# One-hots of every third tile made by ScalarE, and another order of the node products, in a graph layer

## The reference

```python
h = relu(layernorm(x))
skip_s, skip_v = s(h) @ W_skip0, v(h) @ W_skip1          # per node
s1, v1 = s(h) @ W_nl0, v(h) @ W_nl1
w = relu(edge_feat @ W_fc1) @ W_fc2                      # per edge, 224 weights
tp = products of w, s1[dst], v1[dst], direction          # per edge
agg = segment_sum(tp, src) / 32                          # per node
out_s = agg_s @ W_out_s + skip_s
out_v = agg_v @ W_out_v + skip_v
out = x + [silu(out_s[:, :64]), sigmoid(out_s[:, 64:]) * out_v]
```

## Time and profile before

| | us |
|---|---|
| median of 3 runs (1141.44 to 1143.91) | 1142.42 |
| profiled execution | 1140.97 |
| its span, first to last instruction | 1139.1 |
| PE busy | 1092.1 (96%) |
| DVE busy | 978.3 (86%) |
| ACT busy | 865.4 (76%) |
| POOL busy | 777.3 (68%) |

### The profile page before, as it was taken

One profiled execution on the slowest core, in us unless ns is written; L12 is line 12 of the kernel. 1 busy time (PEld: TensorE's weight loads), 2 busy tenths in 40 slices (PEclk: granted clock), 3 DMA queues, 4 the chain that ended last, 5 costly groups with the idle time before them and its releaser, 6 DMA issues.

```text
span 1139.1 us, 29582 instructions
## 1 busy us (share of the span) xinstructions
PE 1092.1 (96%) x8847; PEld 930.7 (82%) x8847; DVE 978.3 (86%) x3574; ACT 865.4 (76%) x2069; POOL 777.3 (68%) x1021
## 2 busy tenths in 40 slices
PE   6889899999999999888899999999999999999996
PEld 5667688888888888777788888888888888888885
DVE  9999889888888898776498998999989989899974
ACT  0400377877877877555899999999999999999994
POOL 6777777777777777776456767666676666767650
PEclk9899899999999999788799999999999999999998
DMA  9999545555545675334578887878888878887863
GB/s 340 403 404 402 207 130 139 138 139 138 137 140 137 211 239 149 110 113 116 176 291 283 298 288 287 291 290 288 300 288 287 290 289 289 300 289 287 290 217 110
DMA packets 108460, 271.13 MB, mean 238 GB/s; under 512 B 13573, under 2 KB 51751, under 8 KB 108364
## 3 DMA queue, kind: packets, MB, share of 16 engines
q1 hardware_dynamic: 87852, 233.20, 58.3%
q0 software_dynamic: 19200, 36.48, 10.5%
q10 hardware_dynamic: 1312, 0.29, 0.1%
HBM read 126.91 MB, written 143.01 MB: 237 GB/s over the span
## 4 chain that ended last, share of the span: by engine, by line
PE 82%; DVE 8%; issue 3%; DMA 3%; POOL 2%; ACT 0%; SPq 0%; ACTq 0%; DVEq 0%; POOLq 0%
PE bank L1482 18%; PE bank L1495 12%; PE bank L1474 11%; PE bank L1411 6%; PE bank L1486 6%; PE bank L1440 4%; PE bank L1344 4%; PE bank L1312 3%; PE bank L1428 3%; PE bank L1424 3%; PE bank L1426 3%; PE bank L1448 2%; PE bank L1394 2%; DVE bin_hot L644 2%; DVE rank_junk L717 2%
## 5 line engine op out<-in xcount | busy, mean ns | idle before, releaser
L1261 ACT ACTIVATE nn<-xb,n_bias,n_rstd 128x160 f32<-128x160 f32 x784 | 344.9, 522 | 0.0
L530 POOL DMA_INDIRECT slots<-msg,sidx x200 | 209.8, 1049 | 68.3 <-issue 55.0
L979 DVE BATCH_NORM_STATS2 n_stat<-xb 128x6 f32<-128x160 f32 x784 | 195.2, 310 | 12.4 <-DMA xb<-x 10.9
L1070 DVE SCALAR_TENSOR_TENSOR ob<-sg,bank 128x128 f32<-128x128 f32 x588 | 131.9, 279 | 58.3 <-ACT ob L1276 57.2
L1495 PE MATMUL bank<-mg,hot 64*128 64x192 f32 x1568 | 171.8, 338 | 3.1 <-DVE hot L1055 3.1
L514 POOL DMA_INDIRECT xg<-x,dst_i x136 | 135.6, 997 | 44.1 <-issue 42.0
L1268 ACT ACTIVATE nt<-bank 128x640 f32<-128x640 f32 x196 | 137.7, 703 | 33.1 <-PE bank L1475 25.4
L579 POOL TENSOR_TENSOR n_rstd<-n_sum,neg_half 128x8 f32<-128x8 f32 x94 | 156.5, 1665 | 7.6 <-POOL n_sum L572 6.9
L1474 PE MATMUL bank<-ident,nn 128*128 128x128 f32 x784 | 146.8, 310 | 2.6 <-ACT nn L1261 2.6
L1077 DVE TENSOR_TENSOR ob<-ob,xb 128x1280 f32<-128x1280 f32 x98 | 146.3, 1493 | 3.4
L1474 PEld LDWEIGHTS bank<-ident,nn 128*128 128x128 f32 x784 | 109.0, 207 | 47.0 <-issue 46.3
(11 more groups left out here) (194 smaller groups left out, 2680.5 us busy)
## 6 DMA issues: line engine op xcount, KB each, us to landing
xb<-x SPq DMA_DIRECT2D x97, 640.0 KB, 5.2
out_dram<-ob SPq DMA_DIRECT2D x97, 640.0 KB, 3.3
slots<-blank SPq DMA_DIRECT2D x14, 2744.0 KB
mg<-slots SPq DMA_DIRECT2D x98, 392.0 KB, 4.0
messages<-msg SPq DMA_DIRECT2D x50, 382.8 KB
ef<-edge_feat_t SPq DMA_DIRECT2D x50, 125.0 KB, 2.3
slots<-msg,sidx POOLq DMA_INDIRECT x200, 3.8
xg<-x,dst_i POOLq DMA_INDIRECT x136, 6.7
```

The costliest lines, as they stand in the source:

```text
L530: pool.indirect_dma_start(slots[:, :], bass.IndirectOffsetOnAxis(ap=sidx[:, m:m + 1], axis=0), msg[:, c, t, 0:MW], None).then_inc(e_sc[c], 16)
L979: done = dve.bn_stats(n_stat[:, u // U, u % U * G + g, :], xb[:, u, g, :])
L1261: last = act.activation(nn[:, u % 2, h, spread_of(g % 4)], xb[:, u, g, order_of(g % 4)], ACT.Relu, bias=n_bias[:, u // U, c:c + 1], scale= ...
```

## The change

Three parts. **Binning:** the one-hots of tiles t >= 54 with t divisible by 3 are made by ScalarE: |iota - bin| into a small ring `bin_far`, then relu(weight - weight * that) into `bin_hot`, with a wait for its own first step between. TensorE waits for `b_lit` for these tiles and counts `b_hot` for the others. ScalarE's calls (`lights`) are spread between its other work, and the zero copies to `msg` are moved behind the first group's normalisation, one between every three tiles. `s_half` is merged into `s_blank`.

**Nodes, TensorE:** `skip` is split into the long products (`skip`) and the short ones (`skip_z`). A round becomes turn(i, 1), skip(i, 0), turn(i+1, 0), skip_z(i, 0), add(i, 0), skip_z(i, 1), add(i, 1), skip(i, 1). In half 1 the short products open the sums and the long ones end them.

**Nodes, ScalarE:** `evacuate(i + 1, 0)` goes ahead of `gates(i, 0)`. The copy of half 0 waits for the short products of the macro-tile before (`n.last`), that of half 1 for `n.z`.

```diff
             place -= XO
             return xb[:, place // 2, place % 2 * GE:place % 2 * GE + GE, :]
+        def on_scalar(t):
+
+            return t >= LIT and t % 3 == 0
+
+        def lit_by(t):
+
+            return len([k for k in range(t + 1) if on_scalar(k)])
+
+        def hot_by(t):
+            return t + 1 - lit_by(t)
+
         def within(q):
             return 0 <= q < NG
...
-                pool.wait_ge(s_half, 1)
+                pool.wait_ge(s_blank, 3)
...
-                dve.memset(neg_half[:], -0.5).then_inc(s_half, 1)
+                dve.memset(neg_half[:], -0.5).then_inc(s_blank, 1)
...
-                    if t + AHEAD < NT:
+                    if t + AHEAD < NT and not on_scalar(t + AHEAD):
...
                     act.dma_start(to, of).then_inc(s_w, 16)
                 act.wait_ge(s_tab, 1)
                 act.activation(vec_r[:], vec_d2[:], ACT.Sqrt).then_inc(s_sqrt, 1)
-                act.wait_ge(s_blank, 2)
-                for c in range(MR):
-                    last = act.activation(msg[96:P, c, :, :], blank[96:P, :].rearrange("p (t c) -> p t c", t=GE), ACT.Copy)
-                last.then_inc(s_msgpad, 1)
+                act.wait_ge(b_hot, 1)
+                act.activation(weight_neg[:], weight[:], ACT.Copy, scale=-1.0).then_inc(b_far, 1)
+
+                def lights(first, last):
+
+                    for t in range(first, last):
+                        if on_scalar(t):
+                            k = lit_by(t)
+                            act.wait_ge(b_pre, t - BR + 4)
+                            act.activation(bin_far[:, k % 2, :], iota_bin[0:ET, :], ACT.Abs, bias=bin_of[:, t:t + 1],
+                                           scale=-1.0).then_inc(b_far, 1)
+                            act.wait_ge(b_far, k + 1)
+                            act.activation(bin_hot[:, t % BR, :], bin_far[:, k % 2, :], ACT.Relu, bias=weight[:, t:t + 1],
+                                           scale=weight_neg[:, t:t + 1]).then_inc(b_lit, 1)
+
                 act.wait_ge(s_w, 16 * len(weight_loads))
                 act.activation(fwd[:, SG:WA + WZ], fwd[:, SG:WA + WZ], ACT.Copy, scale=0.5).then_inc(s_fwd, 1)
+                lights(LIT, 66)
                 act.activation(wo_s[:], wo_s[:], ACT.Copy, scale=1.0 / 32.0)
                 act.activation(wo_u[0:S, :], wo_u[0:S, :], ACT.Copy, scale=3.0 ** 0.5 / 64.0)
                 act.activation(wo_u[S:S + V, :], wo_u[S:S + V, :], ACT.Copy, scale=1.0 / 64.0)
                 act.activation(wo_u[S + V:S + 2 * V, :], wo_u[S + V:S + 2 * V, :], ACT.Copy, scale=1.5 ** 0.5 / 64.0)
+                lights(66, 75)
                 for j in range(2):
                     same, cross = slice(2 * V * j, 2 * V * j + V), slice(2 * V * j + V, 2 * V * j + 2 * V)
                     act.activation(wo_v[same, :], wo_v[same, :], ACT.Copy, scale=1.0 / 64.0)
...
                         last.then_inc(e_norm, 1)
                 root_e(0)
-                norm_e(0, range(GE))
+                lights(75, 96)
+                norm_e(0, range(0, 2))
+                lights(96, 99)
+                norm_e(0, range(2, GE))
+                lights(99, 102)
                 act.wait_ge(s_mir, 1)
                 act.activation(rev[:], p_rev, ACT.Copy).then_inc(s_rev, 1)
+                act.wait_ge(s_blank, 2)
+                for c in range(MR):
+                    lights(102 + 3 * c, 105 + 3 * c)
+                    last = act.activation(msg[96:P, c, :, :], blank[96:P, :].rearrange("p (t c) -> p t c", t=GE), ACT.Copy)
+                last.then_inc(s_msgpad, 1)
                 act.wait_ge(e_t, 1)
                 act.activation(ht[:, 0, :, :], f_t, ACT.Copy).then_inc(e_ht, 1)
+                lights(126, 147)
                 act.wait_ge(e_h1, 1)
                 act.activation(hid[:], f_h, ACT.Relu).then_inc(e_hid, 1)
+                lights(147, 165)
                 act.wait_ge(e_w, 1)
                 act.activation(w_sb[:, 0, :, :], f_w, ACT.Copy).then_inc(e_wsb, 1)
+                lights(165, NT)
                 def round_e(q):
                     c = q % 2
...
                     def evacuate(i, h):
                         act.wait_ge(n.t, 2 * i + h + 1)
-                        wait(act, n.z, 2 * i + h - 1)
+                        if h == 0:
+                            wait(act, n.last, 4 * (i - 1) + 2)
+                        else:
+                            wait(act, n.z, 2 * i)
                         act.activation(nt[:, h, :], q_t[h], ACT.Relu).then_inc(n.ht, 1)
                     def gates(i, u, h):
...
                         evacuate(i, 1)
                         if macro_exists(i + 1):
                             norm(i + 1, (u + 1) % XU, 1)
-                        gates(i, u, 0)
                         if macro_exists(i + 1):
                             evacuate(i + 1, 0)
+                        gates(i, u, 0)
                         if macro_exists(i + 2):
                             norm(i + 2, (u + 2) % XU, 0)
...
                 count(2, ones_h, 1)
                 count(2, tri_before, 2).then_inc(b_pre, 1)
                 for t in range(NT):
-                    if t + 3 < NT:
-                        pe.wait_ge(b_hot, t + 4)
+                    if t + 3 < NT and on_scalar(t + 3):
+                        pe.wait_ge(b_lit, lit_by(t + 3))
+                    elif t + 3 < NT:
+                        pe.wait_ge(b_hot, hot_by(t + 3))
                     pe.wait_ge(b_rank, t + 1)
                     if t + 3 < NT:
                         count(t, tri_rest, t)
...
                         pe.transpose(q_t[h][:, 4 * P:5 * P], nn[:, u % 2, h, LAST], ident[:]).then_inc(n.t, 1)
                     def skip(i, h):
-                        z = q_z[h]
                         pe.wait_ge(n.ht, 2 * i + h + 1)
                         wait(pe, n.mul, 2 * i + h - 1)
                         for t in range(4):
-                            pe.matmul(z[:, t, 0:F], nt[:, h, t * P:(t + 1) * P], sides[t // 2][:, skip_cols], start=(t % 2 == 0),
-                                      stop=False, skip_group_check=True)
+                            last = pe.matmul(q_z[h][:, t, 0:F], nt[:, h, t * P:(t + 1) * P], sides[t // 2][:, skip_cols],
+                                             start=(h == 0 and t % 2 == 0), stop=(h == 1), skip_group_check=True)
+                        return last
+
+                    def skip_z(i, h):
+                        pe.wait_ge(n.ht, 2 * i + h + 1)
+                        wait(pe, n.mul, 2 * i + h - 1)
                         for j in range(2):
                             part = slice(HALF * j, HALF * j + HALF)
-                            pe.matmul(z[:, 2 * j:2 * j + 2, F:Z], nt[part, h, 4 * P:5 * P], sides[j][part, skip_z_cols],
-                                      start=False, stop=every, skip_group_check=True)
+                            pe.matmul(q_z[h][:, 2 * j:2 * j + 2, F:Z], nt[part, h, 4 * P:5 * P], sides[j][part, skip_z_cols],
+                                      start=(h == 1), stop=every, skip_group_check=True).then_inc(n.last, 1)
                     def add(i, u, h):
                         pe.wait_ge(n.hot, i + 1)
...
                             slots = slice(CAP * (t // 2), CAP * (t // 2) + CAP)
                             pair = 2 * h + t % 2
                             last = pe.matmul(q_z[h][:, t, 0:Z], hot[slots, u % 2, pair, :], mg[slots, u % U, pair, 0:Z],
-                                             start=False, stop=True, skip_group_check=True)
-                        last.then_inc(n.z, 1)
+                                             start=False, stop=(h == 0), skip_group_check=True)
+                        return last
                     def add_every(i):
...
                     turn(0, 0, 0)
                     def round_n(i, u):
+
                         turn(i, u, 1)
                         skip(i, 0)
-                        if not every:
-                            add(i, u, 0)
                         if macro_exists(i + 1):
                             turn(i + 1, (u + 1) % XU, 0)
-                        skip(i, 1)
+                        skip_z(i, 0)
+                        if not every:
+                            add(i, u, 0).then_inc(n.z, 1)
+                        skip_z(i, 1)
+                        if not every:
+                            add(i, u, 1)
+                        last = skip(i, 1)
                         if every:
                             add_every(i)
                         else:
-                            add(i, u, 1)
+                            last.then_inc(n.z, 1)
                     macros(pe, round_n)
```

More of the change, by code:

```diff
@@ L49, in gnn_layer @@
     BR, AHEAD, ACCS = 20, 6, 3
+    LIT = 54
     MW = 196
@@ L210, in gnn_layer @@
         s_held = sem("s_held")
-        s_half = sem("s_half")
         b_hot = sem("b_hot")
+        b_far = sem("b_far")
+        b_lit = sem("b_lit")
         b_pre = sem("b_pre")
```

(1 more changed line is left out.)

2 lines of the change are left out of this document (added).

## The result

The changed kernel takes **1112.63 us** (median of 4 runs, 1111.03 to 1115.19) against 1141.93 for the kernel before on the same chip (1139.14 to 1143.91): a ratio of 0.9747, 95% interval 0.9717 to 0.9778. The forecast was 1119, in a band of 1113 to 1130, with a range of 1108 to 1134. The profiled execution took 1114.05 us, its span is 1112.2. A second measurement on another chip gave 1116.91 beside 1142.17, ratio 0.9760 (0.9733 to 0.9787); what lies between the two is taken up with the experiments.

A forecast was written before the change was run, and what follows sets the result against it. GpSimd's transfers bound the edge stage's end, TensorE the node stage, next the loads of x. Savings of 18.5, 2.4, about 2 and 0.7 us, together 23.6, off 1140.97 gave 1117.4, against the median 1119; range 1108 to 1134.

The forecast's parts named there:

- The bound of the edge stage: Edge stage: its end hangs on GpSimd's count of transfers, 1.33 us each, not on when binning ends.
- Zero was the term: Binning: 0 us of the 12 us taken off VectorE reach the total; plus or minus 3 us for TensorE's clock.
- TensorE's gain: Node stage: one change into and out of half-height products per macro-tile instead of two, 0.30 us saved, 5.59 us left.
- I take a value between, 0.30 us: Node stage, TensorE: saving per macro-tile chosen between 0.24 us and the weight loader's standing still, 0.40 us a half.
- The sum of 0.24: Node stage, TensorE: lower bound of the saving, 0.10 us into the K=64 products plus 0.14 out of them.
- the ring: Node stage: residual, load of x, statistics, residual; 11.18 us for two macro-tiles, 5.59 to 5.67 each, 5.64 taken.
- Rival A: Node stage: the ring never binds, loads land in 4.9 us or overlap better, TensorE sets the pace; 1105 to 1113, 13%.
- C: Node stage: the ring lengthens, landings 5.4 to 5.5 us or issue held back, 5.75 to 5.83 a macro-tile; 1130 to 1137, 13%.
- D: Node stage: slower, the ring stays at 6.13 us a macro-tile as in the early stretch; 1155 us, 8%.
- ScalarE's order: Node stage: moving the copy ahead of half 0's gates and its new waits cost zero; if any, 0.1 us a macro-tile.
- The rate of transfers: Node stage: at 358 GB/s a macro-tile's transfers take an estimated 4.8 us and bind nothing; the trace shows delay, not rate.

The follow-up runs named there:

- binning alone: Only the binning hunks of the change, put on the kernel before, nodes in the old order: 1141.56 us, ratio 0.9983.
- both further edits: Changed kernel with VectorE's statistics five macro-tiles ahead, not six, and GpSimd taking three gathers a round, not two: 1087.57 us; with the old binning 1087.1.
- the ring open: Changed kernel with VectorE taking node statistics five macro-tiles ahead instead of six (five-ahead), loads issued as before: 1098.82 us, ratio 0.9598.

## Why the prediction was right

**The bound of the edge stage: right.** 151 one-hots are left on VectorE, the last rank starts at 113.6 us, the last gather goes out at 481.21. VectorE's waits for gathered rows grew from 15.3 us to 23.7 in the same stretch; they took up most of what binning gained. The lines (GpSimd's timeline, then groups by line as the earlier trace rows):

```profile
481.21 0.97 POOL L530 DMA_INDIRECT xg<-x,dst_i  x1 [0.30 <-issue]
```

```profile
L672 DVE BATCH_NORM_STATS2 e_stat<-xg 125x6 f32<-125x160 f32 x136 | 36.9, 311 | 23.7 <-DMA xg<-x,dst_i 23.7
```

This isn't chance: the waits are 15.0 to 19.5 us in four kernels with the old binning, 23.7 to 27.8 in seven with the new. Zero was the term, and two comparisons bear it out: binning alone, and both further edits with and without it. But GpSimd's count tells the last gather, not the end: behind it the last 40 scatters took 4 to 11 us more than GpSimd's own 53, and the end moved with that, about as far as the prediction's plus or minus 3 us allowed. One size was off besides: a pair of ScalarE's activations was put at 1.2 us (bounds 1.0 to 1.4). It takes 0.93, by the starts of two pairs in ScalarE's timeline:

```profile
85.35 0.44 ACT L1191 ACTIVATE bin_far<-iota_bin,bin_of 125x196 f16<-125x196 f16 x1
85.83 0.55 ACT L1194 ACTIVATE bin_hot<-bin_far,weight,weight_neg 125x196 f16<-125x196 f16 x1
86.28 0.44 ACT L1191 ACTIVATE bin_far<-iota_bin,bin_of 125x196 f16<-125x196 f16 x1
```

The nearest row, a normalisation of 160 columns, was too dear a model for it. The estimate of 0.89 us from the Trainium skill (ScalarE: Activation LUTs, "What ACT_TABLE_LOAD costs") is the nearer one. Following or ignoring the Trainium skill's advice to leave such work to VectorE (same page, "Rules for kernel authors") made no difference to the time, 1087.1 and 1087.57 us, as the trace's view of a free engine had it.

**TensorE's gain: right in kind, undersized.** The step that failed is "I take a value between, 0.30 us: not all of the loader's standing delays a product". All of it does: 0.40 measured, and 0.40 a half was the loader's waiting. The sum of 0.24 from the earlier trace rows had two of the four places, the step into the short products and the slow first products behind the adds. It missed the first short product's own delay, and the adds' last step was named there but given too little. TensorE alone makes 5.47 us, outside the 5.49 to 5.65 given for it. Had the ring not bound, this step would have cost the forecast its range: with the ring open the kernel takes 1098.82.

**The ring: right, and it is why the error above cost little.** The prediction took 5.64 between the ring's terms (5.59 to 5.67). It gave TensorE 5.59 too, so that the number alone couldn't have told the two apart; the runs with the ring open and lengthened do. The period was 5.626 and 5.651 in two profiles, with VectorE waiting for x in 43 and 52 of 76 macro-tiles, near the "last about half the time" of the prediction. TensorE's true 5.47 is hidden behind it. The middle macro-tiles gave 0.267 each instead of 0.25, the last ten 0.27 each where eight at 0.30 stood, the first 16 and the start 3.1 us together where 2.7 stood. Rival A failed on the other condition: the loads land in 5.15 us, not in 4.9, and hence TensorE's speed can't show. Its time, 1105 to 1113, holds the measured 1112.6 all the same, by another path: a ring at 5.63 plus 2 us of the edge stage. Rivals C and D needed landings over 5.4 us; the medians stayed at 5.15 and 5.2. The one edit that did lengthen the landing, the load put first, lengthens the period as C had it, to 5.719.

**From 1119 to 1112.6.** The node stage gave 24.9 us of span against 23.6 forecast. The edge stage's end added 2.0 where zero, plus or minus 3, was written; in the second measurement, with a first `mg` load at 549.70, the whole gain was 25.3 us. Another 2.4 is the choice of the profiled execution: before, it lay 1.0 below the median that the changed kernel is compared with, after, 1.4 above its own. The last half us is that median itself, 1141.93 where the forecast started from 1142.42. So some 5 of the 6 us come from the edge stage's end and from which executions are compared, not from the node stage.

**ScalarE's order: half right.** Little is late that wasn't before: between 650 and 1080 us the copy waits 3.3 us in 9 places for the short products, and TensorE's long products 3.0 us in 13 for VectorE's gate products, where zero was put. With the ring open neither wait is left. That the place itself may bring 0.05 to 0.07 us a macro-tile was not seen.

**The rate of transfers.** The Trainium skill's 358 GB/s (DMA: Bandwidth & Descriptors, "Specifications") is not contradicted: the five-ahead kernel moves 306 GB/s from 650 to 1080 us. But by that rate nothing would have waited for x, and VectorE did. The ring was a matter of delay, as the prediction weighed it.

## What to carry to other kernels

When the bound engine gets faster, add up every ring that passes through a buffer's reuse (release, issue, landing, use, release) and divide by the items it spans; where that quotient lies just below today's period, it may be the next bound, though no engine's busy share shows it. Here the cure was not an earlier issue, which lengthened the landings, but one more item in the ring: a shift by one macro-tile was worth nothing before the grouping and 18 us with it. And work taken off one engine counts only as far as the next stage waits for it: the count of GpSimd's transfers since the start, times 1.33 us, told the last gather to 2.5 us in ten of the eleven kernels with two gathers a round (to 4 in the other), whatever the binning did.

## What the runs showed of the hardware that was not expected

- The order of issue changes how long transfers issued close together take to land. With the load of x first instead of last, all three landed later: x 6.7 us after its issue instead of 5.1, `mg` 8.0 instead of 4.0, the store 7.7 instead of 3.3, at the same GB/s (299 and 300) and with the DMA engines 0.92 instead of 0.83 busy. In the kernel before, the load of x went the same way, to 6.5.
- A passage from 128-row to 64-row products and back costs TensorE at four places, about 0.1 us at each: the step into the first short product, that product, the step out of the last adds, and the first long products. Short products that follow adds of 64 rows take 0.05 us from one to the next where the first of a group takes 0.16.
- With the same code in it, the edge stage ended anywhere from 543.7 to 549.7 us in seven profiles, and the total moved with it. In 481 to 510 us the granted clock was 0.70 and 0.72 in the two latest and 0.88 in the two soonest, but at 0.82 stand 545.2 as well as 549.0.
